# Graph layer on one core: float32r source rows, three heads of the gathered row added by TensorE, and p's bias and split moved

## The reference

```python
feats = jnp.maximum(x @ w1 + bb1, 0.0) @ w2 + bb2          # per head: 256 -> 256 -> 64
x_cat = jnp.concatenate([feats[row], feats[col], elem[:, None]], axis=1)   # 129 wide
hid = jnp.maximum(x_cat @ a1 + aab1, 0.0)                  # 129 -> 129
e1 = jax.nn.leaky_relu((hid @ a2 + aab2)[:, 0], negative_slope=0.2)
w = jnp.exp(e1 - jnp.max(e1))
pooled = jax.ops.segment_sum(w[:, None] * feats[col], row, num_segments=n)
row_sum = jax.ops.segment_sum(w, row, num_segments=n) + 1e-10
h = pooled / row_sum[:, None]
out = layernorm(x + concat_heads(h))
```

## Time and profile before

| | |
|---|---|
| time, median of 3 runs | 4868.68 us (4866.79 to 4869.52) |
| span of the profiled execution | 4828.3 us, so 40.4 us under the median lie around it |
| busy, share of the span | DVE 92%, PE 88%, ACT 79%, Pool 56% |
| sort and node stage | 25 groups of about 52.6 us (1000 us hold 19 of them) |
| edge stage | 208 super-blocks of about 15.08 us |
| mean granted TensorE clock | 0.977 |

### The profile page before, as it was taken

One profiled execution on the slowest core, in us unless ns is written; L12 is line 12 of the kernel. 1 busy time (PEld: TensorE's weight loads), 2 busy tenths in 40 slices (PEclk: granted clock), 3 DMA queues, 4 the chain that ended last, 5 costly groups with the idle time before them and its releaser, 6 DMA issues.

```text
span 4828.3 us, 133194 instructions
## 1 busy us (share of the span) xinstructions
PE 4260.4 (88%) x24114; PEld 3004.1 (62%) x24115; DVE 4460.2 (92%) x25378; ACT 3835.5 (79%) x12983; POOL 2693.5 (56%) x2886
## 2 busy tenths in 40 slices
PE   1598998898896999999999999999999999999990
PEld 1355555555555777777777777777777777777760
DVE  8799999999996999999999999999999999999998
ACT  1587778778774888888888888888888888888884
POOL 5366666666664555555555555555555555555544
PEclk9999999999997999999999999999999999999995
DMA  2133333333334877777777777777777777777757
GB/s 85 43 73 86 79 71 80 81 77 80 79 76 137 240 225 221 228 225 224 224 225 224 225 225 221 226 224 224 225 224 224 224 225 225 225 225 225 221 172 212
DMA packets 266918, 851.82 MB, mean 176 GB/s; under 512 B 107916, under 2 KB 109584, under 8 KB 266861
## 3 DMA queue, kind: packets, MB, share of 16 engines
q0 software_dynamic: 169920, 673.54, 50.0%
q1 hardware_dynamic: 63543, 160.18, 11.2%
q10 hardware_dynamic: 33398, 17.49, 1.4%
HBM read 739.10 MB, written 111.90 MB: 176 GB/s over the span
## 4 chain that ended last, share of the span: by engine, by line
PE 36%; ACT 27%; issue 3%; DVE 2%; DMA 1%; ACTq 0%; POOL 0%; DVEq 0%; SPq 0%; POOLq 0%
ACT z L1164 18%; PE psum L971 15%; PE psum L975 9%; PE psum L958 8%; ACT onehot L1193 3%; ACT onehot_t L1182 3%; PE psum L984 3%; ACT onehot L1197 2%; PE psum L939 1%; DVE z L1689 1%; DVE z L1682 0%; PE psum L995 0%; ACT onehot L1195 0%; DVE z L1705 0%; DMA p_win<-p_table 0%
## 5 line engine op out<-in xcount | busy, mean ns | idle before, releaser
L754 POOL DMA_INDIRECT z<-qf_table,rec x1664 | 1609.2, 967 | 1454.9 <-PE psum L958 1027.1
L1164 ACT ACTIVATE z<-z 128x64 f32<-128x64 f32 x6656 | 1651.1, 335 | 0.0
L971 PE MATMUL psum<-p_win,onehot_t 128*128 x9984 | 1407.8, 274 | 84.1 <-ACT onehot_t L1182 68.3
L971 PEld LDWEIGHTS psum<-p_win,onehot_t 128*128 128x128 bf16 x9984 | 966.8, 97 | 540.0 <-issue 214.4
L958 PE MATMUL psum<-z,onehot 128*128 128x260 f32 x3328 | 1029.4, 391 | 6.7 <-DVE acc L1617 4.9
L975 PE MATMUL psum<-z,ident 128*128 128x258 f32 x3328 | 1002.7, 383 | 0.0
L1568 DVE SCALAR_TENSOR_TENSOR z<-z,a_b 128x129 f32<-128x129 f32 x3328 | 884.3, 290 | 5.6 <-issue 0.2
L1568 DVE SCALAR_TENSOR_TENSOR z<-psum,a_b 128x129 f32<-128x129 f32 x3328 | 828.2, 286 | 0.0
L1558 DVE TENSOR_TENSOR z<-z,psum 128x258 f32<-128x258 f32 x1664 | 698.6, 420 | 94.6 <-PE psum L975 90.6
L1617 DVE TENSOR_TENSOR acc<-acc,psum 125x260 f32 x1664 | 702.3, 422 | 25.3 <-PE psum L958 2.4
L695 POOL DMA_INDIRECT sorted_rows<-z x300 | 478.5, 1595 | 403.9 <-DVE z L1447 321.6
(11 more groups left out here) (220 smaller groups left out, 5576.3 us busy)
## 6 DMA issues: line engine op xcount, KB each, us to landing
p_table<-acc SPq DMA_DIRECT2D x100, 338.6 KB
p_win<-p_table SPq DMA_DIRECT2D x100, 338.6 KB
z<-qf_table,rec POOLq DMA_INDIRECT x1664, 4.5
qf_table<-acc SPq DMA_DIRECT2D x75, 339.5 KB
acc<-in_x_dram SPq DMA_DIRECT2D x25, 448.0 KB
z<-in_x_dram SPq DMA_DIRECT2D x20, 560.0 KB
out_dram<-z ACTq DMA_DIRECT2D x20, 560.0 KB
qf_table<-z SPq DMA_DIRECT2D x25, 339.5 KB
```

Of the source, the lines that this page charges most:

```text
L754: pool.indirect_dma_start(out=z_t[:, o + j, :], out_offset=None, in_=qf_table, in_offset=bass.IndirectOffsetOnAxis(ap=rec[:, o + j, 3:4].b ...
L971: mm = pe.matmul(to, onehot_t[:, j, :], p_flat[:, bass.ds((w % 2) * (3 * ZW) + (part * ZW + o), n)], start=(part == 0), stop=(part == 2 an ...
L1164: op = act.activation(z_t[:, slot, o:o + DO], z_t[:, slot, o:o + DO], ACT.Copy, scale=z_t[:, slot, o + DO:o + HF])
```

## The change

- p is kept as two float32r parts instead of three bf16 parts: `p_table` rows go from 3 x 516 bf16 (3096 bytes) to 2 x 516 float32 (4128 bytes), `p_win` and the transposed one-hots `onehot_t` are float32r, and a tile has 4 float32r matmuls of 258 columns instead of 6 bf16 ones.
- `PEH` goes from 2 to 3: the gathered row of head 1 is also added by PE, through the identity (float32, 129 columns). DVE's add is 129 wide instead of 258. Three of the four dot products now read PSUM.
- In the node stage the bias is added by PE: two matmuls with three rows of contraction, bf16, 258 columns, ahead of each p product. ACT takes the sum out of PSUM as the first part (`take_p`), DVE makes the second part as PSUM minus the first (`p_rest`). `p_sum` and Pool's `split_p` are gone. DVE's quarters for this are 12, 14, 0 and 2 of the next group, instead of 11, 13, 15 and 1.
- The bias row is split in three bf16 parts by five Pool instructions on one partition, ahead of Pool's part in the histogram, and SP waits for them before it clears `sorted_rows`.
- The window tables move to a partition of the accumulator that the sums don't use; SP copies them there with one DMA between the bulk and the edge stage.
- Some constants and one-hots of the histogram lie elsewhere.

```diff
-    PEH = 2
-    NA = (H - PEH) * AT if PEH else HALF
-    NB = ZW - NA
+    PEH = 3
+    NV = (H - PEH) * AT
...
-        p_win = sb("p_win", [P, 2, 3 * ZW], BF16)
+        p_win = sb("p_win", [P, 2, 2 * ZW], F32R)
...
-        onehot_t = sb("onehot_t", [P, SB, P], BF16)
+        onehot_t = sb("onehot_t", [P, SB, P], F32R)
...
+            sp.wait_ge(s_ab_step, 5)
+            for u in range(3):
+                sp.dma_start(ab1_rows[u:u + 1, :], ab1_parts[0:1, u * ZW:(u + 1) * ZW]).then_inc(s_ab_rows, 16)
             sp.wait_ge(s_empty, 1)
...
+            sp.wait_ge(s_acc_zero, 1 + BULK)
+            sp.dma_start(tables, made).then_inc(s_tab_st, 16)
+            sp.wait_ge(s_tab_st, 16)
...
+            pool.tensor_copy(bp[:, 0, :], br).then_inc(s_ab_step, 1)
+            pool.wait_ge(s_ab_step, 1)
+            pool.tensor_tensor(rest, br, bp[:, 0, :], ALU.subtract).then_inc(s_ab_step, 1)
...
-            def split_p(g, w):
...
                 if w == 0:
                     pe.wait_ge(s_f_ev, g * 2 + 2)
-                since(pe, s_p_ev, n)
+                since(pe, s_p_lo, n)
                 for q in range(2):
-                    mm = pe.matmul(psum[0:WN, 5 + q, 0:HALF], f_t[:, q, at], ad_p[:, q, :], start=True, stop=True)
+                    pe.matmul(psum[0:WN, 5 + q, 0:HALF], ones_b[0:3, 0:WN], ab1_rows[0:3, q * HALF:(q + 1) * HALF], start=True, stop=False)
+                for q in range(2):
+                    mm = pe.matmul(psum[0:WN, 5 + q, 0:HALF], f_t[:, q, at], ad_p[:, q, :], start=False, stop=True)
...
-                    for o, n, to in ((0, NA, z_one(slot)), (NA, NB, z_two(slot))):
-                        for part in range(3):
-                            mm = pe.matmul(to, onehot_t[:, j, :], p_flat[:, bass.ds((w % 2) * (3 * ZW) + (part * ZW + o), n)],
...
+                    for o, to in ((0, z_one(slot)), (HALF, z_two(slot))):
+                        for part in range(2):
+                            pe.matmul(to, onehot_t[:, j, :], p_flat[:, bass.ds((w % 2) * (2 * ZW) + (part * ZW + o), HALF)],
+                                      start=(part == 0), stop=False, skip_group_check=True)
+                    pe.wait_ge(s_gather[slot], i * 16 + 16)
+                    pe.matmul(z_one(slot)[:, NV:HALF], ident[:, :], z_t[:, slot, NV:HALF], start=False, stop=True, skip_group_check=True)
+                    mm = pe.matmul(z_two(slot), ident[:, :], z_t[:, slot, HALF:ZW], start=False, stop=True, skip_group_check=True)
...
+            def take_p(g, w):
+                n = g * 4 + w
+                act.wait_ge(s_p_mm, n + 1)
+                since(act, s_p_st[w % 2], g * 64 + w // 2 * 32)
+                act.activation(p_out[0:WN, w % 2, 0:ZW].bitcast(F32R).rearrange("p (q n) -> p q n", q=2), psum[0:WN, 5:7, 0:HALF], ACT.Copy).then_inc(s_p_hi, 1)
...
-            beside = {11: [(0, p_sum, 0)], 13: [(0, p_sum, 1)], 15: [(0, p_sum, 2)], 1: [(-1, p_sum, 3)]}
+            def p_rest(g, w):
+
+                dve.wait_ge(s_p_hi, g * 4 + w + 1)
+                dve.tensor_tensor(p_out[0:WN, w % 2, ZW:2 * ZW].bitcast(F32R).rearrange("p (q n) -> p q n", q=2), psum[0:WN, 5:7, 0:HALF],
+                                  p_out[0:WN, w % 2, 0:ZW].rearrange("p (q n) -> p q n", q=2), ALU.subtract).then_inc(s_p_lo, 1)
+
+            beside = {12: [(0, p_rest, 0)], 14: [(0, p_rest, 1)], 0: [(-1, p_rest, 2)], 2: [(-1, p_rest, 3)]}
...
-                        own = z_t[:, slot, 0:NA]
-                        dve.tensor_tensor(own, own, z_one(slot), ALU.add).then_inc(s_z_added, 1)
...
+                    own = z_t[:, slot, 0:NV]
+                    dve.tensor_tensor(own, own, z_one(slot)[:, 0:NV], ALU.add).then_inc(s_z_added, 1)
```

More of the change, by code:

```diff
@@ L27 @@
 BF16 = mybir.dt.bfloat16
+F32R = mybir.dt.float32r
 AX_X = mybir.AxisListType.X
@@ L697, in scatter @@
                         in_=rows_out[0:KB[k], (b - 3) % 2, 2 * (W + 1) + k * SF:2 * (W + 1) + (k + 1) * SF], in_offset=None, compute_op=ALU.add).then_inc(s_scat, 16)
-            def split_p(g, w):
[L701 to L716, removed]
             def group(g):
-                for work, off, n in order:
-                    if work is scatter and isinstance(g, int) and g * PER + n - 3 == BLOCKS - 1:
+                for n in range(PER):
+                    if isinstance(g, int) and g * PER + n - 3 == BLOCKS - 1:
                         pool.wait_ge(s_sum, 4 * BLOCKS)
                         pool.iota(win_iota, [[P, NT]], base=0, channel_multiplier=0, allow_small_or_imprecise_dtypes=True).then_inc(s_win_iota, 1)
-                    if (live_b(g, n, -3) if work is scatter else not isinstance(g, int) or 0 <= g + off < GROUPS):
-                        work(g + off, n)
+                    if live_b(g, n, -3):
+                        scatter(g, n)
             sort_loop(pool, group)
@@ L863, in feats @@
                 if m == 0:
[L864 removed]
+                    since(pe, s_p_lo, g * 4)
                 pe.wait_ge(s_h_ev, g * MC + m + 1)
@@ L1121, in group @@
                         take_rows(g, b)
-                    for work, *args in beside.get(q, []):
-                        if not isinstance(g, int) or g < GROUPS:
-                            work(g, *args)
+                    for off, work, *args in beside.get(q, []):
+                        if not isinstance(g, int) or 0 <= g + off < GROUPS:
+                            work(g + off, *args)
             act.dma_start(base_rows_d[:, :, :].rearrange("h u n -> h (u n)"), base_hl[0:BLOCKS, :].bitcast(BF16)).then_inc(s_base_st, 16)
@@ L1555, in add_rows @@
                     dve.wait_ge(s_z_mm, tile(0, j) + 2)
-                    if PEH:
-                        own = z_t[:, slot, 0:NA]
-                        dve.tensor_tensor(own, own, z_one(slot), ALU.add).then_inc(s_z_added, 1)
-                        for h in range(H - PEH, H):
-                            op = dot(slot, h, z_two(slot)[:, h * AT - NA:(h + 1) * AT - NA])
-                        op.then_inc(s_z_free, 1)
-                    else:
-                        own = z_t[:, slot, 0:ZW].rearrange("p (q n) -> p q n", q=2)
-                        dve.tensor_tensor(own, own, psum[:, slot % 2 * 2:slot % 2 * 2 + 2, 0:HALF], ALU.add).then_inc(s_z_free, 1)
+                    own = z_t[:, slot, 0:NV]
+                    dve.tensor_tensor(own, own, z_one(slot)[:, 0:NV], ALU.add).then_inc(s_z_added, 1)
+                    for h in range(H - PEH, H):
+                        half = (z_one(slot), z_two(slot))[h // 2]
+                        op = dot(slot, h, half[:, h % 2 * AT:(h % 2 + 1) * AT])
+                    op.then_inc(s_z_free, 1)
                 def dot(slot, h, of):
@@ L1573, in own_dot @@
                     if h == 0:
-                        dve.wait_ge(s_z_added if PEH else s_z_free, tile(0, j) + 1)
+                        dve.wait_ge(s_z_added, tile(0, j) + 1)
                     op = dot(slot, h, z_t[:, slot, h * AT:(h + 1) * AT])
```

130 lines of the change are left out of this document (67 added, 63 removed).

## The result

The changed kernel takes 4955.2 us (median of 4 runs, 4952.2 to 4958.1), beside 4869.1 us (4866.8 to 4870.2) for the kernel before: ratio 1.0178, 95% interval 1.0164 to 1.0193. The prediction was 4877, and its range ended at 4930.

What follows compares the result with a forecast made beforehand. It took a loop of ACT and PE to bound the edges, and in the sort DVE slowed by Pool's splits, then a PE-DVE loop. 4828.3 + 10 - 5 + 4 - 3 + 2 = 4836, plus 40.4: 4877 us; range 4800 to 4930.

Steps and rivals of the forecast that it cites:

- Step 6: Sort stage: `p_rest` one quarter later makes PE wait before product 3; 52.4 us a group, -5 us in 25 groups.
- Rival D: Sort stage: late `p_rest` costs more than Pool's split did; 53.3 to 54 us a group, 4910 us in all; chance 0.15.
- part 5: Sort stage: without Pool's split, and if nothing else changed, a group falls from 52.6 to about 48.5 us.
- The signs of being wrong: Edge and sort stages: super-blocks under 14.9 us, float32r matmuls over 0.12 us apart, or groups under 51 us.
- Step 1: Edge stage, PE: four float32r matmuls at the bf16 price replace six bf16 ones, saving 0.23 us a tile.
- rival A: Edge stage: float32r isn't as cheap as bf16; at 0.22 us a matmul +500 us, 5370 us; chance 0.12.
- Steps 2 to 4: Edge stage: head 1 on PE 0.22 us a tile; DVE's half-width add gains 0 on the path; 4-byte eviction costs 0.
- Step 7: Sort stage: ACT's four `take_p` evictions, each about 0.5 us, cost 0; up to 1 us a group if a store delays them.
- Steps 8 and 9: Before the sort, Pool's bias instructions +4 us; around the bulk, last blocks without splits -3 us, table DMA +2 us.

Runs made afterwards that it cites:

- the first trace of before: The unchanged kernel's profile that the prediction was made from: span 4828.3 us, beside a measured median of 4868.7 us.
- the second trace of before: The unchanged kernel profiled once more, with no edit: span 4874.7 us, time 4875.6 us.
- `p_rest` early: The changed kernel with all four of VectorE's `p_rest` moved back to quarters 11, 13, 15 and 1: 4821.4 us, ratio 0.989 to the kernel before.
- the narrow add: The kernel before with VectorE's add of the source rows cut from 258 columns to 129: 4873.2 us, ratio 1.000.
- only `p_rest` 2 early: The changed kernel with only `p_rest` 2 moved back, from quarter 0 to quarter 15: 4821.0 us, ratio 0.989 to the kernel before.
- the first experiment: The kernel before, run and profiled again without any edit: 4875.6 us, ratio 1.000.
- The nine of the experiments: The nine follow-up kernels, each timed beside the kernel before: the unchanged one again and edits of it or of the changed kernel, 4705.0 to 4986.0 us.

## Why the prediction was wrong, step by step

The sum went by the first trace of before, whose 40.4 us "around the span" aren't around it: in every other trace, time and span lie some 2 us apart, and the second trace of before has the rest inside, at the edges. 4828.3 + 40.4 is the measured median by construction, so this step did no harm to the time. It would have, had only the two traces been compared: the changed kernel would then seem to lose 74 us at the edges, where it loses 29.

- **Step 6, the late `p_rest`, is the one that failed; its mechanism is right and its size is off.** "Together 51.65 us", "53.3 with low clock", "I take 52.4" a group, so -5 us; measured 54.62 against 52.4, +55 us over 25 groups. From PE's product 3 to the prefix of quarter 12 the trace has 37.5 us (881.20 to 918.68), not 35.1: PE is busy in all but 0.2 of it, so this part is PE's own work. With `p_rest` early the same stretch is 35.4 us (857.92 to 893.32). So 2.1 of the 2.4 us are the lower clock right behind the wait, by the starts: bias 0.61 instead of 0.37, product 1.88 instead of 0.97, `hidden` 2.72 instead of 1.79. The prediction had read that loss as 1.6 and booked half of it. It took it from one pair of groups of the kernel before, where the lower clock comes in 15 groups of 24; the changed kernel has it in all of them. DVE's part is 17.1 us (918.68 to 935.82) instead of 16.55 with its hand-overs. Rival D, at "53.3 to 54 us a group" and 0.15, was the case, and still too cheap by 0.6.
- **Two smaller things in step 6.** The group of before was put at 52.6 us (1000 us with 19 groups); from group to group it is 52.4 in both traces, which alone is 5 us of the forecast. And the step compared the new loop with the kernel before, where a few tenths of difference look like "no change". That is right for the forecast, but against the 48.5 of part 5 (measured 48.96) the same loop is a loss of 3 to 5 us a group.
- **The signs of being wrong** that the prediction named (super-blocks under 14.9 us, float32r matmuls over 0.12 us apart, groups under 51 us) all stayed away. None of them looked at groups that get longer; of what was to be seen, groups of 51.6 to 53.3 us is the line that was missed.
- **Step 5, Pool's split goes:** right. The `chunks` of four are back at 0.94 us for the most part (one has a mean of 302 ns, in before some 387), and with the wait away the group is 48.96 us, predicted 48.5.
- **Step 1, float32r at the bf16 price:** 0.12 us instead of 0.11 (bounds 0.11 to 0.43), and a weight load of 189 ns. This is the other mis-sized term: +29 us at the edges instead of +10. The Trainium skill ("TensorE: Matmul & The Clock Gate", Weight-path perf modes), weighed in the prediction, would have given 19 for the load alone; the trace agrees with it, 189 against 97 ns. The 0.01 us on each of the loop's 12 matmuls would be 25 us more. Together that is more than the 29 measured; how the loop gets some of it back no run shows. The 0.125 us from which rival A was to tell was nearly reached.
- **Steps 2 to 4** hold: head 1 on PE 0.22 us a tile; ACT's eviction to float32r 597 ns in the median as to bf16; DVE's relief is worth nothing on the path, shown by the narrow add.
- **Step 7** (`take_p`) holds in so far as only `p_rest` 2 early brings the whole gain with `take_p` in place. DVE then waits for it, 49.4 us in 21 waits from 400 to 1400 us with all four early, beside the path.
- **Steps 8 and 9:** the first prefix starts at 168.83, 3.7 us later than the 165.16 of the second trace of before (+4 predicted); from there to the last prefix the 55.2 us come, nearly all of them step 6; the blocks after the last group gave -6 instead of -3, the table DMA +0.5 instead of +2.

The sum again, with the measured terms: 4874.7 + 3.7 + 55.2 - 6.3 + 0.5 + 29.1 - 0.9 = 4956.0, beside a span of 4955.9. The time was missed by 78 us: 60 are step 6, 19 step 1, -6 the other terms, and some 5 the difference between traces and times told with the first experiment.

## What to carry to other kernels

When work is moved one place down an in-order queue, look at what stands in the place that it passes, and at who waits: four instructions were moved here, three cost nothing, and the one that went behind the heaviest stretch cost 136 us. Compare a new loop with what the change would reach without it, not with the kernel before, or a gain that is eaten looks like no change. A wait of TensorE can cost more than itself: here 3.5 us of idle time brought 2.1 us of slower matmuls behind them, in each group, and one group of a trace doesn't tell how often that happens. And a busy share of 93% proved to be no bound; the closed loop in the chain of waits was.

## What was not expected of the hardware

- The executions of one program differ in places: of two traces of the kernel before only one has ACT waiting 18.0 us at the start of the edge stage for what the profile calls "remote". The nine of the experiments and the changed kernel all take 46.6 to 49.1 us for the first two super-blocks, 21 to 24 us more than the other trace of before. In the changed kernel's trace the last matmuls of PE's fourth tile are recorded at 1621.04, and DVE begins with their result at 1633.08. The cause is open.
- The same traces have a short stall, of some 0.6 to 2.6 us, every 11 or 12 super-blocks at the edges. In the changed kernel one such eviction is

```profile
2703.37 0.60 ACT L1201 ACTIVATE onehot_t<-psum 128x512 fp32r<-128x512 f32 x1 [4.05 <-remote]
```

where it waited 2.26 us for PE one super-block earlier. The stalls go by the number of the super-block and not by time: numbers 36, 81, 92, 126, 137, 171 and 182, counted from 0, are over 0.5 us longer than the median in all ten traces that have such stalls, with a median of 14.7 us as of 15.24. What they come from no run here took apart.
- A float32r matmul of 258 columns costs 0.12 us from start to start, against 0.11 for bf16 and 0.22 for each of the two instructions of a float32 one; its weights load at the float32 price, 189 ns.
